# Issue order in the pipelined slots of an audio tower: the second layer, scores 2 and 3, and the exponentials

## The reference

```python
p = patchify(x)                                   # 32 patches of 64*16 values for each series
h = relu(p @ W1 + b1) @ W2 + b2                   # layer 1, layer 2
h = h + attn(layernorm(h))                        # 16 heads, 32 tokens; ternary weights, 8-bit activations:
#     q, k, v = bitlinear(x, w_q / w_k / w_v); softmax(q k^T / 4) v; bitlinear(., w_o)
h = h + ffn_top1(layernorm(h))                    # one expert matrix, gate and capacity of 100 per gate
h = h + ssm(layernorm(h))                         # a complex linear recurrence along the 32 tokens
h = h + moe_top2(layernorm(h))                    # 8 experts, 256 -> 512 -> 256, silu(x M1) * (x M2) @ M3
```

## Time and profile before

| | |
|---|---|
| median of 3 runs | 541.97 us (541.93 to 542.85) |
| the profiled execution's own time | 543.37 us |
| its span, first to last instruction | 541.3 us |
| TensorE busy in the span | 435.5 us, 80% |
| VectorE busy | 304.0 us, 56% |
| ScalarE busy | 199.5 us, 37% |
| GpSimd busy | 162.1 us, 30% |
| mean granted TensorE clock | 0.907 of full speed |

### The profile page before, as it was taken

One profiled execution on the slowest core, in us unless ns is written; L12 is line 12 of the kernel. 1 busy time (PEld: TensorE's weight loads), 2 busy tenths in 40 slices (PEclk: granted clock), 3 DMA queues, 4 the chain that ended last, 5 costly groups with the idle time before them and its releaser, 6 DMA issues.

```text
span 541.3 us, 9169 instructions
## 1 busy us (share of the span) xinstructions
PE 435.5 (80%) x3291; PEld 283.5 (52%) x3292; DVE 304.0 (56%) x869; ACT 199.5 (37%) x369; POOL 162.1 (30%) x140
## 2 busy tenths in 40 slices
PE   0699798788666855637759999999799999999991
PEld 0254445446464643535535766676565666566661
DVE  0596778674698899998897577726431111111110
ACT  0234453444465523113322653245323233223321
POOL 6041010020011023531041545354244343354422
PEclk9999999979976956765679999999999999999997
DMA  9999010063045100343110422243132325332321
GB/s 177 247 211 200 1 42 2 18 201 137 10 121 226 27 19 2 134 178 115 41 30 21 117 39 41 40 117 46 25 48 43 55 39 150 82 56 41 45 24 19
DMA packets 36102, 43.14 MB, mean 80 GB/s; under 512 B 5216, under 2 KB 30560, under 8 KB 35904
## 3 DMA queue, kind: packets, MB, share of 16 engines
q1 hardware_dynamic: 26384, 32.14, 21.3%
q0 software_dynamic: 7488, 10.23, 12.3%
q10 hardware_dynamic: 2192, 0.27, 0.5%
HBM read 30.96 MB, written 11.53 MB: 78 GB/s over the span
## 4 chain that ended last, share of the span: by engine, by line
PE 56%; DVE 23%; DMA 7%; issue 7%; ACT 3%; SPq 1%; POOL 1%; POOLq 0%; DVEq 0%; ACTq 0%
PE psum L2011 21%; PE psum L2030 11%; PE psum L1714 7%; DMA KT<-in_L_attn_w_o_dram 3%; PE psum L2021 3%; PE psum L1727 2%; PE psum L1739 2%; DMA out_dram<-mixture_rows_out 2%; PE psum L1752 2%; PE psum L2001 1%; DVE st_att L989 1%; DMA KT<-mixture_rows_in,src_i 1%; DVE mx L1023 1%; DVE st_in L989 1%; PE psum L1843 1%
## 5 line engine op out<-in xcount | busy, mean ns | idle before, releaser
L1616 DVE TENSOR_TENSOR QT<-QT,psum 128x512 f32<-128x512 f32 x39 | 26.8, 687 | 134.8 <-PE psum L2011 134.6
L1714 PE MATMUL psum<-M2s,M1s 128*128 128x512 f32 x128 | 62.3, 643 | 19.1 <-DMA M1s<-in_L_tok_W_dram 18.7
L2011 PE MATMUL psum<-M1s,KT 128*128 x156 | 75.5, 607 | 1.2 <-issue 0.6
L2030 PE MATMUL psum<-M3s,KT 128*128 x312 | 74.2, 381 | 1.5 <-ACT KT L788 0.8
L2011 PE MATMUL psum<-M2s,KT 128*128 x156 | 73.3, 592 | 0.0
L2030 PEld LDWEIGHTS psum<-M3s,KT 128*128 128x128 f32 x312 | 58.5, 190 | 22.0 <-issue 15.9
L799 ACT ACTIVATE O<-psum,gate_slot 128x256 f32<-128x256 f32 x39 | 18.5, 473 | 108.8 <-PE psum L2030 105.9
L502 POOL DMA_INDIRECT KT<-mixture_rows_in,src_i x39 | 41.0, 1051 | 44.3 <-issue 23.4
L1714 PEld LDWEIGHTS psum<-M2s,M1s 128*128 128x128 f32 x128 | 25.7, 206 | 49.5 <-issue 30.4
L2011 PEld LDWEIGHTS psum<-M2s,KT 128*128 128x128 f32 x156 | 29.8, 191 | 37.6 <-issue 37.6
L529 POOL DMA_INDIRECT mixture_rows_out<-O,src_i x17 | 31.6, 1858 | 31.4 <-ACT O L799 12.6
(11 more groups left out here) (398 smaller groups left out, 732.4 us busy)
## 6 DMA issues: line engine op xcount, KB each, us to landing
M3s<-in_x_dram SPq DMA_DIRECT2D x4, 1024.0 KB, 10.7
M3s<-in_L_ffn_W_dram SPq DMA_DIRECT2D x1, 4096.0 KB, 14.6
M2s<-in_L_ffn_W_dram SPq DMA_DIRECT2D x1, 4096.0 KB, 14.7
M1s<-in_L_ffn_W_dram SPq DMA_DIRECT2D x1, 4096.0 KB, 14.2
M3s<-in_x_dram SPq DMA_DIRECT2D x4, 992.0 KB, 14.5
M1s<-vtok SPq DMA_DIRECT2D x64, 34.0 KB, 1.9
mixture_rows_out<-H SPq DMA_DIRECT2D x4, 512.0 KB, 4.4
M1s<-in_L_tok_W_dram SPq DMA_DIRECT2D x2, 512.0 KB, 14.3
```

What stands on the lines that cost most here:

```text
L1616: v.tensor_tensor(sil[:, u, :], sil[:, u, :], bank[3], ALU.mult).then_inc(v_gated, 1)
L1714: last = mm(bank[6 + c], W1s[:, r, P * c:P * (c + 1)], xr[:, i % 2, r].rearrange("p b l -> p (b l)"), start=(n == 0), stop=(n == STRIDE - 1))
L2011: last = mm(z, xrT[:, u, c, :], w[:, bass.ds(e, 1), c, :].rearrange("p a h -> p (a h)"), start=(c == 0), stop=(c == CH - 1))
L2030: last = mm(bank[6][:, 0:DM], actT[:, u, c, :], M3s[:, bass.ds(e, 1), c, :].rearrange("p a d -> p (a d)"), start=(c == 0), stop=(c == HC - 1))
```

## The change

Nothing is computed in another way; only the order of statements changes.

- TensorE: `scores` of batches 2 and 3 come directly after `layer1(iA, slot, 1)`. `layer2` stays there in slot 0 only. In slots 1 and 2 (stage B, no stage D: `layer2_last`) it comes after the q, k, v matmuls and ahead of `values`; in slot 3 it comes after the transposes of `oq` and `xq` and ahead of `att_proj`. The wait for the ternary weights' copies moves up to the `xq` transposes.
- ScalarE: `hidden(1)` comes behind the quantisation of stage B's rows, where both are there (slot 3). The `H` evictions come after the q, k, v evictions in slots 1 and 2; in slots 0 and 3 they stay where they were. The exponentials of batches 2 and 3 come ahead of the q, k, v evictions in slots 2 and 3, and stay behind them in slots 4 and 5.
- VectorE: `sort_x` and `ssm_tables` come behind `turn` of batches 0 and 1 and `minus_max` of batches 2 and 3. Only slot 2 has both.

```diff
--- before.py
+++ after.py
@@ -650,19 +650,24 @@
                     r.then_inc(a_att_quant, 1)
                 if iC is not None:
                     exps(iC, range(0, 2))
-                if iA is not None and iA > 0:
-                    hidden(1)
                 if together:
                     act.wait_ge(v_scales, iB + 1)
                     for t in range(TS):
                         r = a.activation(x1[:, t, :], x1[:, t, :], ACT.Copy, bias=MAGIC, scale=SB1["s"][:, t:t + 1])
                     r.then_inc(a_in_quant, 1)
-                if iA is not None:
+                if iA is not None and iA > 0:
+                    hidden(1)
+
+                def embed(i):
                     for k in range(2):
-                        act.wait_ge(p_layer2, TS * iA + 2 * (k + 1))
-                        r = a.activation(H[:, TS * iA + 2 * k:TS * iA + 2 * k + 2, :].rearrange("p t d -> p (t d)"),
+                        act.wait_ge(p_layer2, TS * i + 2 * (k + 1))
+                        r = a.activation(H[:, TS * i + 2 * k:TS * i + 2 * k + 2, :].rearrange("p t d -> p (t d)"),
                                          bank[6 + k], ACT.Copy)
                     r.then_inc(a_embed, 1)
+
+                layer2_last = iB is not None and iD is None
+                if iA is not None and not layer2_last:
+                    embed(iA)
                 if iA == 0:
                     for c in range(CH):
                         act.wait_ge(p_ternaryT, c + 1)
@@ -674,6 +679,8 @@
                     act.wait_ge(p_xqT, iB + 1)
                     wait(act, p_qkv, TS * iB)
                     a.activation(xqT[:].rearrange("p c n -> p (c n)"), bank[4].bitcast(BF16), ACT.Copy).then_inc(a_xqT, 1)
+                if iC is not None and iN is None:
+                    exps(iC, range(2, BT))
                 if iB is not None:
                     act.wait_ge(v_scales, iB + 1)
                     wait(act, v_qk, iB)
@@ -689,7 +696,9 @@
                         a.activation(vtok[:, t, :, 0:HD],
                                      bank[(2, 4)[t % 2]][:, 0:DM].rearrange("p (h d) -> p h d", d=HD),
                                      ACT.Copy, scale=SB1["sw"][:, 2, t:t + 1]).then_inc(a_qkv, 1)
-                if iC is not None:
+                if iA is not None and layer2_last:
+                    embed(iA)
+                if iC is not None and iN is not None:
                     exps(iC, range(2, BT))
                 if iN is not None:
                     wait(act, p_norm3T, iN)
@@ -1261,11 +1270,6 @@
                     wait(dve, p_xqT, iB)
                     v.tensor_scalar(xq[:], x1[:], MAGIC, 127.0, ALU.subtract, ALU.min).then_inc(v_xq_rows, 1)
 
-                if iA is not None and iA + 1 < STEPS:
-                    sort_x(iA + 1)
-                if iB == 0:
-                    ssm_tables()
-
                 if iN is not None:
                     expert_added(iN, bank[6])
                 if iS is not None:
@@ -1279,6 +1283,11 @@
                     turn(iC, 1)
                     minus_max(iC, 2)
                     minus_max(iC, 3)
+
+                if iA is not None and iA + 1 < STEPS:
+                    sort_x(iA + 1)
+                if iB == 0:
+                    ssm_tables()
 
                 if iN is not None:
                     answered()
@@ -1868,6 +1877,10 @@
                     scores(iC, slot, range(0, 2))
                 if iA is not None:
                     layer1(iA, slot, 1)
+                layer2_last = iB is not None and iD is None
+                if iC is not None:
+                    scores(iC, slot, range(2, BT))
+                if iA == 0:
                     layer2(iA)
                 if iA == 0:
 
@@ -1878,25 +1891,25 @@
                                 last = tr(bank[4 + c].bitcast(BF16)[:, DM * w + P * o:DM * w + P * (o + 1)],
                                           wter[:, w, o, P * c:P * (c + 1)], ident_b[:])
                         last.then_inc(p_ternaryT, 1)
-                if iC is not None:
-                    scores(iC, slot, range(2, BT))
                 if iD is not None:
                     att_columns(iD)
                 if iB is not None:
+                    if iB == 0:
+                        pe.wait_ge(a_ternaryT, CH)
                     pe.wait_ge(v_xq_rows, iB + 1)
                     for c in range(CH):
                         for t in range(TS):
                             last = tr(bank[4].bitcast(BF16)[:, SN * c + P * t:SN * c + P * (t + 1)],
                                       xq[:, t, P * c:P * (c + 1)], ident_b[:])
                     last.then_inc(p_xqT, 1)
+                if iA is not None and iA > 0 and not layer2_last:
+                    layer2(iA)
                 if iD is not None:
                     wait(pe, a_embed, done(slot, A_LAG))
                     wait(pe, a_expert, TS * done(slot - 1, D_LAG))
                     wait(pe, v_kept, done(slot, N_LAG))
                     att_proj(iD)
                 if iB is not None:
-                    if iB == 0:
-                        pe.wait_ge(a_ternaryT, CH)
                     pe.wait_ge(a_xqT, iB + 1)
                     wait(pe, a_oqT, done(slot, D_LAG))
                     pe.wait_ge(v_xq_rows, iB + 1)
```

## The result

The changed kernel runs at 539.82 us (median of 8 runs, 538.08 to 540.78), against 542.96 us for the kernel before (8 runs, 541.93 to 543.71). The ratio is 0.9928, interval 0.9909 to 0.9948: faster, by 0.5 to 0.9% (the two medians alone give 0.9942). Measured a second time beside three other kernels it came to 540.2 us against 541.93, ratio 0.9968, interval 0.9945 to 0.9990. Both say faster, by well under 1%; the intervals overlap only at their ends, and how the size wanders is a part of what follows. The forecast of 0.44% (539.6 against 541.97) lies between the two, just outside the first interval and inside the second.

A forecast was written before the change was run, and what follows sets the result against it. TensorE's own order and its waits were taken to bound the kernel. Gains of 0.6 in slot 1, 1.7 in slot 2 and 0 in slot 3 sum to 2.3 us: median from 541.97 to 539.6, range 536.3 to 541.3.

The forecast's parts named there:

- Slot 1: Layer 2 behind q, k, v in slot 1: scores of batches 0 and 1 start at 73.9, 0.6 us gained.
- Slot 2: Layer 2 of slot 2 hidden almost wholly under the evictions: values start at 95.05, 1.7 us of the sum.
- Slot 3: Saved wait and copy latency in slot 3 pay for the H eviction and exponentials: own gain zero.
- the H eviction in front of the oqT copy: On ScalarE in slot 3, it delays oqT by 0.6 us, to 129.85.
- The exponentials, which I had as a cost here: Two exponentials ahead of slot 3's q, k, v evictions: 1.2 us, evictions start at 133.0.
- The clock in slot 2, "I take zero": A new 1.6 us TensorE gap between slot 2's second and third tile leaves the clock full: cost zero.
- Rival 1: Clock as before in slot 2 but stays up in slot 3: 2.4 and 0.8 us less, 536.4; chance 0.20.
- rival 2: Clock falls briefly in slot 2's new gap, costing 2.5 us: 542.1, no change; chance 0.11.
- rival 3: Clock falls at slot 2's third tile and stays down through layer 2, +4.0 to 4.1 us: 543.7; chance 0.06.
- Rival 4: VectorE's maxima come later, so exponentials hold up the evictions another 1.3 us: 540.9; chance 0.06.
- The rest, "same order, all move": Slots 4 and 5, the tail and the mixture keep their order; the 2.3 us shift stays.

The follow-up runs named there:

- the third experiment: The changed kernel with slot 3's layer 2 between scores 3 and the oq and xq transposes; 539.8 us, ratio 0.9935 to the kernel before.

## Why the prediction was right, and where not

- **Slot 1 (0.6 us):** right, to about 0.1: q, k, v at 57.99 (58.1), layer 1 of step 2 at 66.79 (66.8), scores at 73.94 (73.9). With slot 1 undone 0.6 came back.
- **Slot 2 (1.7 us):** right: evictions from 88.05, layer 2 at 91.05, values at 95.04, each within 0.02. The parts show that the scores ahead of layer 2 bring 0.9, that layer 2 under the evictions (with sort_x moved) brings up to 1.6, and that the early exponentials bring nothing and take 0.7 where the clock stays up.
- **Slot 3 (zero):** right in sum, 0.1 by the trace. The terms inside were right in kind, not in size: the H eviction in front of the oqT copy costs 0.9 where I had 0.6, which the scores moved ahead of layer 2 give back (0.9). The exponentials, which I had as a cost here, cost nothing: from the oqT copy to the first eviction it takes 2.96 us, 2.97 before, since ScalarE waited for the first tile there anyway.
- **The clock in slot 2, "I take zero":** the right value for a reason that failed. I compared gap lengths, 1.6 against 1.41 and 1.56, and said it would stay at full. It fell, about 86.5, before that gap, behind scores, transposes and a wait of 1.12 us. It cost nothing because the first eviction was held up by an exponential anyway: scores to values takes 21.1 us with the fall and 21.1 without. Of the seven profiles with this order of slots 1 and 2, the clock fell there in two (the changed kernel's); in the third experiment's, for one, it did not. The length of a single gap does not decide alone. That the term came out at zero is luck.
- **Rival 1** (slot 3 keeps its clock): it did not happen by shifting; with the wait filled it was worth 3.2 us in slot 3 against a profile with the early fall, the 3.2 I had. In six profiles the fall came later and cost only 1.7, a middle case that I had not listed.
- **Rivals 2 and 3:** a fall came, as in rival 2, but one wait sooner and without its price. The changed kernel's layer 2 in slot 2 took 4.0 us, so rival 3 is out; its kind of fall came in a kernel with a 6.17 us wait, for 0.9 us of layer 2. **Rival 4** did not come.
- **The rest, "same order, all move":** mostly. The shift grew from 2.45 in slot 3 to 2.9 at the start of the mixture and 3.2 at the end of the span, in places that no edit touches. I have not isolated this; the clock differs there between the two profiles (0.83 against 0.79 over the 40 us behind slot 3's values). The clock's falls, here and behind the mixture's pause, are the likely reason why the two ratios differ, 0.9928 and 0.9968, but that was not shown. The forecast was a gain of 2.4 us; between the medians of the two measurements lie 3.1 and 1.7. That it lies 0.2 us from one median is partly luck, since the kernel before ran at 542.96 beside it and not at the 541.97 that I took off from.

## What to carry to other kernels

Put work that nobody waits for into the time in which the evictions are the bound, and look at what stands in front of a copy on the evicting engine: an eviction moved with it can take the gain back (slot 3). When one engine is given an early task, check that the engine that feeds it has been freed as well: the early exponentials without the moved sort_x were slower than the kernel before. Where effects are of the size of one fall of the clock, compare starts in the traces, kernel against kernel, and take more than one profile of the same order: what one fall costs differed by up to 2.9 us between them. Filling a short wait with matmuls is worth a try, with fillers shorter than the wait.

## What was not expected of the hardware

- The granted clock fell in an execution of an order in which it stayed at full in another, in slot 2 (0.83 and 1.00 for the window 84 to 88) and behind the mixture's pause of 2.2 us (1.00, 0.77 and 0.50 for 388 to 392). In these three the same pause cost 0, 1.7 and 2.9 us.
- Useless matmuls that take 1.96 us in a 2.16 us wait shorten the kernel by 2.1 us in the median. The Trainium skill ("TensorE: Matmul & The Clock Gate", section "HAM oscillation — how this bites in real kernels") says that matmul bursts with long enough waits between them restart at the lower clock, and that the cure is to keep the work contiguous. The runs with slot 3's wait filled agree: the clock stayed at 1.00 in all three, and fell in all eleven profiles without. The two profiles with the mixture's pause filled do not speak against it.
- Part of what a spared fall gives was lost again later: 3.4 us at scores 2 of slot 3 were 2.1 at the mixture, 1.2 of them lost in slot 4, where the clock stayed low for longer.
